# One transposing DMA of 128x2048 for two heads in place of one of 128x1024 for each

## The reference

```python
h = jnp.maximum(_layernorm(x, axis=-1), 0.0)
q, k, v = (split_heads(h @ W.T) for W in (Wq, Wk, Wv))       # 16 heads
a = jnp.einsum('bhnd,bhmd->bhnm', q, k) * scale + 2 * adj    # adj is passed as both biases
row_nonzero = jnp.any(a != 0, axis=-1, keepdims=True)
p = jax.nn.softmax(jnp.where(row_nonzero, a, -jnp.inf), axis=-1)
p = jnp.where(jnp.isnan(p), 0.0, p)
o = jnp.einsum('bhnm,bhmd->bhnd', p, v)
out = x + o.transpose(0, 2, 1, 3).reshape(B, N, D) @ Wo.T
```

## Time and profile before

| | |
|---|---|
| median of 3 runs | 1005.39 us (1004.05 to 1005.59) |
| the profiled execution, its own time | 1005.16 us |
| its span | 1003.4 us |
| TensorE busy | 959.6 us (96%) |
| ACT busy | 934.5 us (93%) |
| POOL busy | 862.3 us (86%) |
| DVE busy | 850.0 us (85%) |
| DMA, mean rate | 183 GB/s, 183.62 MB |
| transposing DMAs of probabilities | 512 |

### The profile page before, as it was taken

One profiled execution on the slowest core, in us unless ns is written; L12 is line 12 of the kernel. 1 busy time (PEld: TensorE's weight loads), 2 busy tenths in 40 slices (PEclk: granted clock), 3 DMA queues, 4 the chain that ended last, 5 costly groups with the idle time before them and its releaser, 6 DMA issues.

```text
span 1003.4 us, 33752 instructions
## 1 busy us (share of the span) xinstructions
PE 959.6 (96%) x11580; PEld 660.2 (66%) x11580; DVE 850.0 (85%) x3092; ACT 934.5 (93%) x3049; POOL 862.3 (86%) x936
## 2 busy tenths in 40 slices
PE   5879999999999999999999999999999999999965
PEld 4656776666677666777666677766666776667632
DVE  6778998888989888898988889988889898888863
ACT  5799999999999999999999999999999999999992
POOL 2278998989998898999888899989889988889894
PEclk9989999999999999999999999999999999999979
DMA  6289999999999999999999999999999999999995
GB/s 251 49 148 195 183 190 194 183 193 186 190 191 184 195 178 187 194 199 180 192 177 198 183 203 184 189 194 178 198 183 197 186 191 193 177 185 176 175 175 119
DMA packets 573818, 183.62 MB, mean 183 GB/s; under 512 B 547024, under 2 KB 555216, under 8 KB 573648
## 3 DMA queue, kind: packets, MB, share of 16 engines
q1 hardware_dynamic: 573648, 181.48, 100.9%
HBM read 29.36 MB, written 16.78 MB: 46 GB/s over the span
## 4 chain that ended last, share of the span: by engine, by line
PE 56%; DVE 28%; issue 8%; ACT 5%; POOL 1%; DMA 1%; DVEq 0%; POOLq 0%; ACTq 0%; SPq 0%
PE ps L1045 35%; DVE logits L752 15%; PE ps L1113 9%; PE ps L1063 7%; DVE stats L649 4%; ACT probs L547 3%; PE ps L942 3%; DVE q_lo L815 2%; DVE o_norm L782 2%; PE ps L1089 1%; DVE some L770 1%; ACT p L560 1%; PE ps L1019 1%; DMA w_nat<-in_L_gnn_Wq 1%; DVE row_min L752 1%
## 5 line engine op out<-in xcount | busy, mean ns | idle before, releaser
L430 POOL TENSOR_TENSOR p<-probs,p 128x512 f16<-128x512 f32 x512 | 586.4, 1161 | 89.9 <-ACT p L560 89.7
L547 ACT ACTIVATE probs<-logits,row_min 128x256 f32<-128x256 f32 x1024 | 513.6, 511 | 3.8 <-DVE row_min L752 3.8
L752 DVE CUSTOM_DVE_ANT_0 logits<-ps,adj_s,sigma 128x256 f32<-128x256 f32 x1024 | 438.0, 475 | 7.1 <-PE ps L1063 7.0
L560 ACT ACTIVATE p<-probs 128x512 f16<-128x512 f32 x512 | 323.5, 632 | 0.0
L1045 PE MATMUL ps<-ht_hi,w_hi 128*128 128x256 f16 x1024 | 280.2, 274 | 7.7 <-DVE q_lo L815 2.6
L1045 PE MATMUL ps<-ht_lo,w_hi 128*128 128x256 f16 x1024 | 279.4, 273 | 0.0
L1045 PE MATMUL ps<-ht_hi,w_lo 128*128 128x256 f16 x1024 | 279.4, 273 | 0.0
L547 ACT ACTIVATION_READ_ACCUMULATOR probs<-logits,row_min 128x1 f32 x1024 | 209.8, 205 | 0.0
L1045 PE MATMUL ps<-wo,o_hi 128*128 128x512 f16 x496 | 149.2, 383 | 3.8 <-POOL o_lo L456 3.8
L1045 PEld LDWEIGHTS ps<-ht_hi,w_hi 128*128 128x128 f16 x1024 | 100.1, 98 | 36.1 <-DVE q_lo L815 13.0
L1045 PEld LDWEIGHTS ps<-ht_lo,w_hi 128*128 128x128 f16 x1024 | 100.4, 98 | 14.0
(11 more groups left out here) (90 smaller groups left out, 1571.0 us busy)
## 6 DMA issues: line engine op xcount, KB each, us to landing
xs<-in_x SPq DMA_DIRECT2D x32, 512.0 KB, 4.6
out<-xs SPq DMA_DIRECT2D x64, 256.0 KB, 2.9
adj_raw<-in_adj SPq DMA_DIRECT2D x32, 256.0 KB, 3.2
pt<-p SPq DMA_TRANSPOSE x256, 4.0
w_nat<-p SPq DMA_TRANSPOSE x256, 3.4
w_nat<-in_L_gnn_Wq SPq DMA_DIRECT2D x2, 512.0 KB, 5.4
w_nat<-in_L_gnn_Wk SPq DMA_DIRECT2D x1, 1024.0 KB, 8.3
w_nat<-in_L_gnn_Wv SPq DMA_DIRECT2D x1, 1024.0 KB, 11.3
```

The source lines that it names most:

```text
L430: g.tensor_tensor(p16[:, c % 2, k, 1], probs[:, h % 4].rearrange("p u n -> p (u n)"), p16[:, c % 2, k, 0], ALU.subtract).then_inc(p_split, 1)
L547: e = a.activation(probs[:, h % 4, u, :], logits[:, h % 4, u, :], ACT.Exp, bias=row_min[:, t.par(d), u, h:h + 1], scale=-1.0, accum_out=ro ...
L560: a.activation(p16[:, c % 2, k, 0], probs[:, h % 4].rearrange("p u n -> p (u n)"), ACT.Copy)\
L752: v.tensor_tensor_reduce(out=logits[:, h % 4, u, :], in0=ps[:, S_BANK + h % HC, N * u:N * u + N], in1=adj_s[:, t.par(d), u, :], scale=sigm ...
```

## The change

Two heads, 2j and 2j + 1 of the same group, are transposed by one DMA. turn() does nothing for an even head. For an odd one it waits until this head is split (POOL goes through the heads in order, so the even one is split too), and issues one transpose that reads `p16[:, c % 2, k:k + 2]`, 128 x 2048 fp16 (512 KB), and writes 16 blocks of 128 x 128; `pt_two` names its destination. There are two semaphores per group in place of four. ACT, before it writes over either head's buffer, waits for the pair's transpose; TensorE waits for two per group in place of four.

```diff
--- before.py
+++ after.py
@@ -188,7 +188,7 @@
         pv_done = sem("pv_done")
         p_hi = sem("p_hi")
         p_split = sem("p_split")
-        pt16_in = [[sem(f"pt16_in{i}{k}") for k in range(HC)] for i in range(NC)]
+        pt16_in = [[sem(f"pt16_in{i}{k}") for k in range(HC // 2)] for i in range(NC)]
         v_hi_ready = sem("v_hi_ready")
         rows_tested = sem("rows_tested")
         norm_step = sem("norm_step")
@@ -216,6 +216,12 @@
 
             store = pt16[:, c, k] if c < 2 else w16[:, c - 2, k].rearrange("p (l n) -> p l n", n=P)
             return store
+
+        def pt_two(c, k):
+
+            if c < 2:
+                return pt16[:, c, k:k + 2].rearrange("p k l n -> p (k l) n")
+            return w16[:, c - 2, k:k + 2].rearrange("p k (l n) -> p (k l) n", n=P)
 
         AUX_USES = [("h", 0, 0), ("h", 0, 1)]
         for b in range(-1, NB + 1):
@@ -350,15 +356,15 @@
             def turn(t, s):
 
                 d, h = head(t, s)
-                if d is None or not by_dma(h):
+                if d is None or h % 2 == 0:
                     return
-                c, k = h // HC, h % HC
+                c, k = h // HC, h % HC - 1
 
                 sp.wait_ge(p_split, x_count(t.batch(d), h) + 1)
 
                 need(sp, pv_done, 2 * t.batch(d) + c // 2 - 1)
-                sp.dma_start_transpose(pt(c, k), p16[:, c % 2, k].rearrange("p l n -> p (l n)"))\
-                  .then_inc(pt16_in[c][k], 16)
+                sp.dma_start_transpose(pt_two(c, k), p16[:, c % 2, k:k + 2].rearrange("p k l n -> p (k l n)"))\
+                  .then_inc(pt16_in[c][k // 2], 16)
 
             def slot(t):
                 for s in range(H):
@@ -556,7 +562,7 @@
                 c, k = h // HC, h % HC
                 act.wait_ge(probs_ready, H * t.batch(d) + (h + 1))
 
-                need(act, pt16_in[(c - 2) % NC][k], 16 * (t.batch(d) + c // 2))
+                need(act, pt16_in[(c - 2) % NC][k // 2], 16 * (t.batch(d) + c // 2))
                 a.activation(p16[:, c % 2, k, 0], probs[:, h % 4].rearrange("p u n -> p (u n)"), ACT.Copy)\
                  .then_inc(p_hi, 1)
 
@@ -1103,7 +1109,7 @@
                     for u in range(NU):
                         pe.wait_ge(pj_taken[u], (NJ // 2) * t.batch(d) + 3)
                 for c in (2 * p, 2 * p + 1):
-                    for k in range(HC):
+                    for k in range(HC // 2):
                         pe.wait_ge(pt16_in[c][k], 16 * (t.batch(d) + 1))
                     for mh in range(NU):
                         for j in range(HC):
```

## The result

| | before | changed |
|---|---|---|
| median | 1005.23 us (1004.05 to 1005.81, 16 runs) | 1007.41 us (1004.47 to 1008.46, 16 runs) |
| ratio | | 1.0020, 95% interval 1.0012 to 1.0027 |
| profiled execution, its span | 1005.16, 1003.4 us | 1007.36, 1005.6 us |

The forecast was 1005.4 us with a range of 1002.5 to 1014. The change costs 2.2 us by the medians, 0.22%, which is at the edge of the 0.2% that I called no change. It was run beside two later experiments once more each and gave ratios of 1.0011 (1.0002 to 1.0020) and 1.0019 (1.0010 to 1.0027).

What follows compares the result with a forecast made beforehand. TensorE was taken as the bound, working without a hole in the steady part, every other engine having room. Removed, added and moved terms summed 0 + 0 + 0 + 0, so 1005.4 us, range 1002.5 to 1014.

Steps and rivals of the forecast that it cites:

- rival A: Slower: pair lands after TensorE needs it at group 1; some 1010 us with extra 2.5, 1026 with 4.0; chance 0.17.
- all margins hold: Case in which no engine waits for the later landings; 1003.4 to 1007.4 us, chance 0.72.
- its own sign: Forecast wrong if landing after issue exceeds 8.2 us for heads 6 and 7, or 4.4 in the last batch.
- 256 issues fewer on SP: On SP's queue, 8 issues fewer per batch; SP waits for POOL anyway, so worth nothing.
- Two waits fewer per group: On TensorE before the value products, two semaphore waits in place of four; worth 0 us.
- The size of the extra: Later landing of the odd head from the doubled transfer; taken as 1.24 us, bounds 0 and 4.0.
- (a): TensorE at group 1, head 7: margin 1.7 us becomes 0.5 in worst batch, 3.5 becomes 2.3 usually; no wait.
- (b): TensorE at group 3 of steady batches, head 15: margin 2.7 us becomes 1.5; no wait.
- (d): ACT writing into the buffer used by the head eight before: margin 1.5 us becomes 0.3; no wait.
- (c): Last batch, on the path to the end: landing 4.34 us against 4.42 allowed, 0.1 left; no wait.
- B: Slower: large transposes become the pace, period over 29.50 us; would add 79 us, 1084; chance 0.03.
- C: Faster: fewer transfers and waits give back TensorE's idle time, 3.7 us over 31 batches, 1001.7; chance 0.08.

Runs made afterwards that it cites:

- e6: Changed kernel (all pairs) with each of TensorE's two waits per group written twice, 128 instructions more; 1005.24 us, ratio 1.0005.
- e2: Kernel before (single transposes), only heads 14 and 15 of the last batch turned as a pair; 1005.32 us, ratio 1.0002.
- e1: Changed kernel, but heads 14 and 15 of the last batch turned by two single 256 KB transposes; 1006.16 us, ratio 1.0004.
- e4: Against the changed kernel, one 1 MB transpose per group of four heads in place of pairs; 1071.58 us, ratio 1.068.
- e3: The changed kernel run again, unchanged, with a profile of its own; 1006.36 us, ratio 1.0011.
- e5: Kernel before, with the last head's transpose held back on SP until TensorE turned the last normalizing factors; 1009.57 us, ratio 1.0043.
- e7: Kernel before (single transposes), with 128 more waiting instructions at the start of TensorE's program; 1013.56 us, ratio 1.0087.
- e8: The changed kernel run once more, unchanged, beside the two padded kernels; 1007.05 us, ratio 1.0019.

## Why the prediction was right, and where it was not

The number fell into the range because the steady part behaved as foreseen. The term of the last batch did not, and that the number held in spite of it is in part luck: the top of the range, 1014, had been set for rival A. The forecast gave a range of its own for the case that all margins hold, 1003.4 to 1007.4, and 1007.41 lies at its edge while one margin did not hold. By its own sign, a landing more than 4.4 us after the issue in the last batch, the forecast was wrong there: it was 5.5.

**What bounds the kernel.** Right: the steady part doesn't feel the change, by 705.99 us of TensorE's work against 706.13 and by e6, which has pairs everywhere and the time of before.

**The terms that are nothing.** 256 issues fewer on SP are worth nothing: right. Two waits fewer per group: no time by themselves, right, but not nothing. "No instruction of TensorE, DVE, ACT or POOL moves" was the sentence that failed. The matmuls stay in order; the program that holds them gets shorter, and the fetches of it move. I had not looked at the fetches at all.

**The size of the extra.** I took 1.24 us, with bounds of 0 and 4.0. It is 1.2 where the queue is free, and about 0 behind the load of x in the slow batch at 416 us, the two cases that the prediction told apart; in the middle of the steady batches head 7 lands 0.8 us later after its split, and the pair of heads 0 and 1 takes 7.0 us where head 1 took 3.9, which is more than either and was not foreseen. The issue was put at 2.5 us; the medians are 2.1 and 3.1. The Trainium skill's rate for these transfers ("DMA: Bandwidth & Descriptors", "Latency and other measured facts", 261 GB/s) gave 1.0 us as an estimate; the trace shows 212 GB/s while the pair flows and 1.2 us, so the measurement decides, and it is the slower one.

**The margins.** (a) and (b), the groups 1 and 3 of steady batches, never failed. (d), ACT, did not wait. (c), the last batch: 3.1 + 1.24 = 4.34 us was foreseen, 4.2 and 4.3 were measured in e2 and e6, and the margin held in both. In the changed kernel it failed, by the fetch that added 1.2 to 1.3 us to the pair. Neither alone does it: the pair without the fetch cost no wait (e2, e6), a single with it 0.3 us (e1). So the term that was mis-sized is the extra in the last batch, put at 1.24 us and measured as 5.5 - 3.1 = 2.4; by the prediction's own margin that is a wait of 1.1 us, and it was 1.06 by the idle time in the timeline and 1.24 by the starts of the groups. The prediction had 0.1 us of room there and named it as the place on the path to the end; with so little room I should have asked what else may enter the queue in those 4.4 us.

**The rivals.** A (the pair is late at group 1) didn't occur; its like did, at group 3, for one batch, which the prediction had only as "a little for what the last batch may lose together with a dip of the clock there", under slower at 0.21. B (the pace) and C (faster) did not. e4 shows the direction A would have taken with larger steps: ACT stalls first, not TensorE.

**What is open.** The loss is 2.2 us and the wait 1.1 to 1.24, or none (e3). e5's wait of 2.47 us cost 4.4, so a wait at this place costs more than itself, and the clock after it is the likely rest. But from group 3 to the end it is 9.9 us before and in e3, and 11.1 to 11.6 in all the others but e5, with a wait (e1, e7, e8, changed) and without one (e2, e6), so the lower clock there doesn't need the wait. Against e6, the profiled span of the changed kernel is 1.9 us longer: 0.4 us until group 2, 1.25 for the wait, 0.2 from group 3 on. Where the clock's part comes from stays open. Why one engine's fetch stops nearly all the packets of a transpose isn't shown either, nor why they come back only 0.8 us after the fetch's own packet has ended. The Trainium skill says that a DMA engine changes between its queues only at the end of a packet ("DMA: Bandwidth & Descriptors", "Queues, rings and completion order"); if the fetch of 16 KB sits on one engine and the transpose is spread over several, the transpose would wait for that one. The hole of 1.4 us is in line with a wait of this kind, though longer than the fetch's packet of 0.9 us, and no run here separates it from other reasons.

## What to carry to other kernels

Merging DMAs on a queue that isn't the bound brought nothing here, and its price was the later landing of the last one: look for the place where the pipeline drains, since there is no later work that hides it. A change that removes only semaphore waits still moved the fetches of the program behind it, and a margin of a few tenths of a microsecond in the tail can be lost by that; a padding of idle waits on the same engine, put where other work hides it, tells such an effect from the change itself.

## What the runs showed of the hardware

- A 16 KB fetch of instructions lengthened the transposing DMA that it met by 1.2 to 1.7 us (3.1 to 4.6 and 4.8 us for 256 KB, 4.2 to 5.4 and 5.5 for 512 KB); in the changed kernel's pair there is a hole of 1.4 us at 8 GB/s, between stretches at 212 and 195.
- TensorE's program came in pieces of 16 KB while it ran, one for 255 of its instructions in the mean, and 128 instructions fewer moved the last piece from 981.9 to 991.3 us.
- A transposing DMA between buffers on the chip lands 3.0 us after its issue with 256 KB, 4.2 with 512 KB and 6.7 with 1 MB at the least; the issue holds SP for 1.23 us, 1.3 at the least (2.1 and 3.1 in the middle), and 4.7.
- A semaphore wait that is already met isn't free where nothing hides it: 127 of them stand in e7's trace one every 107 ns, from 1.5 to 15.1 us, and the first matmul came 7.5 us later; the rest of them fell into time in which TensorE waited for its data anyway. In the steady part the same kind of instruction, four waits or two in front of a matmul, made no difference.
